# Layer two's channel norm on one Trainium2 core: centring folded into the dense weights, variance from sums of squares, the deviation spread as two bf16 products

## What is computed

```
def _L2_conv_ref(x, dw_w, dw_b, ln_g, ln_b, w1, b1, w2, b2, ls):
    y = conv7x7_depthwise(x, dw_w) + dw_b
    y = transpose(y, (0, 2, 3, 1))
    mu = mean(y, axis=-1, keepdims=True)
    var = mean(square(y - mu), axis=-1, keepdims=True)
    y = (y - mu) * rsqrt(var + 1e-5) * ln_g + ln_b
    h = gelu(einsum('btfc,hc->btfh', y, w1) + b1)
    y = einsum('btfh,ch->btfc', h, w2) + b2
    return transpose(y * ls, (0, 3, 1, 2))
```

## Time and profile before

| | |
|---|---|
| median of 3 runs | 3942.23 us (3942.04 to 3947.88) |
| the profiled execution's own time | 3944.25 us |
| its span, first to last instruction | 3942.5 us |
| mean granted TensorE clock | 0.941 of 2.4 GHz |
| busy share of the span | PE 87%, DVE 82%, ACT 55%, POOL 55% |
| layer two's stretches (four) | about 613 to 768, 1522 to 1683, 2432 to 2592 and 3341 to 3498 us |

### The profile page before, as it was taken

One profiled execution on the slowest core, in us unless ns is written; L12 is line 12 of the kernel. 1 busy time (PEld: TensorE's weight loads), 2 busy tenths in 40 slices (PEclk: granted clock), 3 DMA queues, 4 the chain that ended last, 5 costly groups with the idle time before them and its releaser, 6 DMA issues.

```text
span 3942.5 us, 78824 instructions
## 1 busy us (share of the span) xinstructions
PE 3422.8 (87%) x29499; PEld 2153.6 (55%) x29499; DVE 3218.1 (82%) x6755; ACT 2180.3 (55%) x4937; POOL 2150.4 (55%) x1888
## 2 busy tenths in 40 slices
PE   4999988989999998989999998988999998983555
PEld 1666643347667753336767753345776763343444
DVE  4999977769999967859999968859999977855666
ACT  2434432348888852338888862347888863232333
POOL 3455552447767523437767704437767715327775
PEclk9999999999999999999999999999999999995556
DMA  1000102065555412055555511045555521137775
GB/s 52 10 12 12 28 18 52 26 188 171 156 156 158 130 39 52 1 170 170 161 152 166 156 48 41 12 134 169 163 159 157 159 69 30 35 106 208 217 216 171
DMA packets 219932, 426.84 MB, mean 108 GB/s; under 512 B 27825, under 2 KB 126540, under 8 KB 217512
## 3 DMA queue, kind: packets, MB, share of 16 engines
q0 software_dynamic: 92160, 302.06, 25.9%
q1 hardware_dynamic: 127346, 119.80, 10.7%
q10 hardware_dynamic: 54, 0.01, 0.0%
HBM read 340.97 MB, written 60.71 MB: 102 GB/s over the span
## 4 chain that ended last, share of the span: by engine, by line
DVE 29%; PE 26%; POOL 8%; issue 7%; ACT 5%; DVEq 3%; SPq 2%; POOLq 0%; DMA 0%; ACTq 0%
DVE val L1331 7%; DVE mxc L1294 6%; DVE xl L1354 6%; PE bank L737 4%; POOL G L1794 4%; PE bank L598 3%; DVE val L1341 2%; PE bank L621 2%; PE bank L459 2%; DVE G L1485 2%; POOL reg L1794 2%; POOL x_cur L1794 1%; PE bank L559 1%; PE bank L811 1%; PE bank L562 1%
## 5 line engine op out<-in xcount | busy, mean ns | idle before, releaser
L1794 POOL DMA_INDIRECT G<-patch_table,idx x576 | 709.2, 1231 | 285.7 <-issue 165.6
L957 ACT ACTIVATE pt<-bank 128x512 f32<-128x512 f32 x1024 | 606.9, 593 | 322.5 <-DVE bank L1362 221.7
L598 PEld LDWEIGHTS bank<-vt,pt 128*128 128x128 bf16 x8192 | 548.1, 98 | 244.1 <-ACT pt L957 6.7
L1354 DVE TENSOR_TENSOR xl<-pt 128x512 bf16<-128x512 f32 (+1 forms) x1024 | 616.8, 603 | 60.4 <-PE bank L598 29.7
L1294 DVE TENSOR_REDUCE mxc<-bank 128x1 f32<-128x512 f32 x896 | 611.4, 684 | 32.2 <-PE bank L520 29.5
L598 PE MATMUL bank<-vt,pt 128*128 128x129 bf16 (+1 forms) x8192 | 633.7, 221 | 1.1 <-ACT osb L965 1.1
L598 PE MATMUL bank<-vt,xl 128*128 128x129 bf16 x4096 | 401.6, 221 | 10.7 <-DVE xl L1354 10.7
L1794 POOL DMA_INDIRECT reg<-patch_table,idx x256 | 302.3, 1181 | 115.5 <-issue 72.5
L1794 POOL DMA_INDIRECT x_cur<-patch_table,idx x256 | 303.2, 1184 | 103.7 <-issue 72.5
L520 PE MATMUL bank<-reg,qh 128*128 128x512 bf16 x896 | 342.2, 383 | 10.4 <-DVE mxc L1294 6.8
L1530 DVE SCALAR_TENSOR_TENSOR G<-xn,vec,G 128x512 f32<-128x512 f32 x384 | 305.0, 832 | 24.8 <-issue 20.4
(11 more groups left out here) (295 smaller groups left out, 7171.1 us busy)
## 6 DMA issues: line engine op xcount, KB each, us to landing
patch_table<-valt SPq DMA_DIRECT2D x64, 512.0 KB, 7.2
G<-patch_table,idx POOLq DMA_INDIRECT x576
x_cur<-in_x SPq DMA_DIRECT2D x4, 2048.0 KB, 8.8
xl<-in_x SPq DMA_DIRECT2D x32, 256.0 KB
attn_out<-ob SPq DMA_DIRECT2D x32, 256.0 KB, 2.9
x_store<-x_cur SPq DMA_DIRECT2D x4, 2048.0 KB, 6.5
xr<-x_store SPq DMA_DIRECT2D x32, 256.0 KB, 4.1
out<-fo SPq DMA_DIRECT2D x32, 256.0 KB
```

What stands on the lines that cost most here:

```text
L598: last = mm(O[t // 2][:, c0:c0 + width], image[:, at % ring, t * 128:(t + 1) * 128], vhl[:, values, st, 0:width], start=(st == 0 and part ...
L957: A(pt[:, at % PT_RING, :], ST[at % ST_RING] if n else ST_FIRST[at % 3], ACT.Exp, scale=SCALE).then_inc(s["exp_done"], 1)
L1354: v.tensor_tensor(pl[:, at % PL_RING, first:CH], pt[:, at % PT_RING, first:CH], ph[:, at % PT_RING, first:CH], ALU.subtract).then_inc(s["p ...
L1794: g.indirect_dma_start(out=patches(j, k), out_offset=None, in_=table[:], in_offset=bass.IndirectOffsetOnAxis(ap=idx[:, j * K1 + k:j * K1 + ...
```

## The change

The mean is no longer subtracted from y. Instead the weights of the first dense layer lose their mean over the input channels, and the conv's bias loses its own mean (setup: two more matmuls with `cavg` on PE, two subtractions on DVE, the scaling by `ln_g` moved ahead). The variance is E[y^2] - E[y]^2: PE makes both sums by one-column float32 matmuls (L760's kind, now eight in a row, at the place where L751 stood), ACT copies the first and squares the second, POOL subtracts, clamps at zero and adds epsilon, takes the power, and splits the 128x4 result in a high and a low bf16 part. ACT makes eight diagonals (bf16) in place of four (float32), and PE spreads them by two bf16 matmuls of 512 columns in place of one float32 one.

```diff
@@ PE, layer2 step
                     if norm:
                         pe.wait_ge(s["y_rdy"], B + 2)
-                        pe.wait_ge(s["ln_d"], B)
-                        mm(MX[0][:], cavg[:], y_chunk(1 - u), start=True, stop=True).then_inc(s["ln_m"], 1)
+                        pe.wait_ge(s["ln_ve"], B)
+                        for t in range(TB):
+                            mm(MX[1][:, TB + t:TB + t + 1], y_chunk(1 - u)[:, t * 128:(t + 1) * 128],
+                               cavg[:, 0:1], start=True, stop=True)
+                        pe.wait_ge(s["ln_sq"], B)
+                        for t in range(TB):
+                            last = mm(MX[1][:, t:t + 1], slots[:, L2SQ + (1 - u), t * 128:(t + 1) * 128],
+                                      cavg[:, 0:1], start=True, stop=True)
+                        last.then_inc(s["ln_v"], 1)
                     if conv:
                         taps(12, 22)
                     elif norm:
                         keep_busy(2, 7)
-                    if norm:
-                        pe.wait_ge(s["ln_sq"], B)
-                        pe.wait_ge(s["ln_ve"], B)
-                        for t in range(TB):
-                            last = mm(MX[1][:, t:t + 1], slots[:, L2SQ + (1 - u), t * 128:(t + 1) * 128],
-                                      cavg[:, 0:1], start=True, stop=True)
-                        last.then_inc(s["ln_v"], 1)
@@
                         pe.wait_ge(s["z_rdy"], B + 1)
-                        mm(TR[1][:], cavg[:], slots[:, L2DG + (1 - u), :], start=True, stop=True)\
+                        mm(TR[1][:], inverse_c, diagonal(1 - u)[:, 0, :], start=True, stop=False)
+                        mm(TR[1][:], inverse_c, diagonal(1 - u)[:, 1, :], start=False, stop=True)\
                             .then_inc(s["ln_bc"], 1)
@@ ACT, layer2 step
-                        act.wait_ge(s["ln_d"], B + 1)
+                        act.wait_ge(s["y_rdy"], B + 2)
                         A(slots[:, L2SQ + (1 - u), :], y_chunk(1 - u), ACT.Square).then_inc(s["ln_sq"], 1)
                     if norm:
                         act.wait_ge(s["ln_v"], B)
-                        A(ve4[:], MX[1][:, 0:TB], ACT.Identity, bias=eps[:]).then_inc(s["ln_ve"], 1)
+                        A(ve4[:], MX[1][:, 0:TB], ACT.Copy)
+                        A(mq4[:], MX[1][:, TB:2 * TB], ACT.Square).then_inc(s["ln_ve"], 1)
                     if norm:
                         act.wait_ge(s["ln_rs"], B)
                         act.wait_ge(s["z_rdy"], B)
-                        for t in range(TB):
-                            last = A(slots[:, L2DG + (1 - u), t * 128:(t + 1) * 128], ident[:], ACT.Copy,
-                                     scale=rs4[:, t:t + 1])
+                        for part, scales in enumerate((rh4, rl4)):
+                            for t in range(TB):
+                                last = A(diagonal(1 - u)[:, part, t * 128:(t + 1) * 128], ident[:], ACT.Copy,
+                                         scale=scales[:, t:t + 1])
                         last.then_inc(s["ln_dg"], 1)
@@ DVE, setup
             v.tensor_copy(xst[0:K1, 0, 0:C], P[1][0:K1, 0:C]).then_inc(s["b2_rows"], 1)
+            v.tensor_scalar(l2w1_s[:], l2w1_s[:], vec[:, LNG:LNG + 1], None, ALU.mult).then_inc(s["w1_scaled"], 1)
@@
-            v.tensor_scalar(l2w1_s[:], l2w1_s[:], vec[:, LNG:LNG + 1], None, ALU.mult)
+            dve.wait_ge(s["w1_mean"], 1)
+            v.tensor_tensor(l2w1_s[:], l2w1_s[:], P[2], ALU.subtract)
+            v.tensor_tensor(vec[:, DWB:DWB + 1], vec[:, DWB:DWB + 1], P[3][:, 0:1], ALU.subtract)
@@ DVE, layer2 step
-                        taps(0, 4)
-                    if norm:
-                        dve.wait_ge(s["ln_m"], B)
-                        v.tensor_tensor(y_chunk(1 - u), y_chunk(1 - u), MX[0][:], ALU.subtract)\
-                            .then_inc(s["ln_d"], 1)
-                    if conv:
-                        taps(4, dve_taps)
+                        taps(0, dve_taps)
@@ POOL, layer2 step
-                    g.tensor_tensor(rs4[:], ve4[:], mhalf[:].to_broadcast([128, TB]), ALU.pow)\
-                        .then_inc(s["ln_rs"], 1)
+                    g.tensor_tensor(ve4[:], ve4[:], mq4[:], ALU.subtract)
+                    pool.drain()
+                    g.tensor_scalar(ve4[:], ve4[:], 0.0, 1e-5, ALU.max, ALU.add)
+                    pool.drain()
+                    g.tensor_tensor(rs4[:], ve4[:], mhalf[:].to_broadcast([128, TB]), ALU.pow)
+                    pool.drain()
+                    g.tensor_copy(rh4[:], rs_high)
+                    g.tensor_tensor(rl4[:], rs4[:], rs_high, ALU.subtract).then_inc(s["ln_rs"], 1)
```

More of the change, by code:

```diff
@@ L110, in build @@
         mhalf = sb("mhalf", [128, 1])
-        eps = sb("eps", [128, 1])
         b1f = sb("b1f", [128, FT])
@@ L145, in build @@
         rs4 = sb("rs4", [128, TB])
+        mq4 = sb("mq4", [128, TB])
+        rh4 = sb("rh4", [128, TB])
+        rl4 = sb("rl4", [128, TB])
         bst = sb("bst", [128, NCH, 6])
@@ L205, in build, with diagonal @@
         tap_eye = w4f[:, 2 * TAP_W:2 * TAP_W + 32]
+        inverse_c = cavg[:].bitcast(BF16)[:, 1::2]
+        rs_high = rs4[:].bitcast(BF16)[:, 1::2]
+        def diagonal(u):
+            return slots[:, L2DG + u, :].bitcast(BF16).rearrange("p (s n) -> p s n", s=2)
         def y_chunk(u):
@@ L297, in build @@
             "t_ps t_ev in_ve in_pow in_ready relu_rdy tl_rdy l1w l1p l1s l1a l1f l1x "
-            "mlp_rdy zl_rdy hl_rdy tapw_in tapw_rdy tapw_out tapw_ld im0 im1 im2 im3 dwp y_rdy ln_m ln_d ln_sq ln_v ln_ve ln_rs ln_dg ln_bc z_rdy hp gl mo me xa "
+            "mlp_rdy zl_rdy hl_rdy tapw_in tapw_rdy tapw_out tapw_ld im0 im1 im2 im3 dwp y_rdy w1_scaled w1_mean ln_sq ln_v ln_ve ln_rs ln_dg ln_bc z_rdy hp gl mo me xa "
             "oc_ps oc_ev ot_ps ot_ev xs_rdy xt_ps xt_ev om_rdy em_rdy grid_rdy idx_rdy x3_out tbl_w "
@@ L453, in _ @@
             nc.tensor.transpose(P[1][0:K1, 0:C], vec[:, L1B:L1B + K1], ident[:]).then_inc(s["pe_setup"], 1)
+            pe.wait_ge(s["w1_scaled"], 1)
+            mm(P[2], cavg[:], l2w1_s[:], start=True, stop=True)
+            mm(P[3][:, 0:1], cavg[:], vec[:, DWB:DWB + 1], start=True, stop=True).then_inc(s["w1_mean"], 1)
             pe.wait_ge(s["dve_setup"], 1)
@@ L1190, in _ @@
             dve.sem_inc(s["y_rdy"], 2)
-            dve.sem_inc(s["ln_d"], 1)
             dve.sem_inc(s["xa"], 2)
@@ L1199, in _ @@
             v.memset(cavg[:], 1.0 / C)
-            v.memset(eps[:], 1e-5)
             dve.drain()
```

## The result

| | before | the changed kernel |
|---|---|---|
| median of 6 runs each | 3943.96 us (3939.08 to 3947.88) | 3960.00 us (3956.70 to 3964.90) |
| ratio to before, 95% interval | | 1.0042 (1.0031 to 1.0052) |
| profiled execution, own time | 3944.25 us | 3962.75 us |
| its span | 3942.5 us | 3961.0 us |
| mean granted TensorE clock | 0.941 | 0.938 |

What follows compares the result with a forecast made beforehand. PE was taken to bound the 17.17 us full step, DVE nearly so. Five full steps at +0.86 (4.3), steps 1 and 2 (0.4) and step 8 (1.1) gave 5.8 us an image, +23 over four: 3965 us, range 3936 to 3983.

Steps and rivals of the forecast that it cites:

- what would show it: Signs: POOL's five instructions about 4 us, PE idle 1 to 2 us before spreading, steps about 18.0, DVE waiting at z.
- POOL starts at 5.26: Full step: sums reach ACT at 4.76 us, two 128x4 instructions follow, then POOL's chain begins at 5.26.
- each link costs a whole tap, about 0.8: Full steps: each drained POOL instruction waits for DVE's tap to end, so each link costs about 0.8 us.
- Eight diagonals: ACT, full step: eight diagonals at 0.30 us each take 2.47 us against 1.28 for four, +1.19.
- PE's own work falls by 0.74: PE, full step: 0.13 us saved on the means and 0.61 on the spreading, 0.74 together.
- The clock falls: Rival: the granted clock drops in the full steps' new wait; given no chance of its own.
- Leave POOL free for the last links: Steps 1 and 2: DVE finishes its taps early, so POOL's last links run free; +0.2 us each.
- Its result matmuls lie under that: Step 8: the uncovered chain grows from 7.43 to 8.5 us, +1.1, and covers the result matmuls.
- The hidden chain: Rival: POOL's links slip between taps, DVE sets the step at 16.6 us, -12 us, 3930; chance 0.2.
- under about 2.6 us: Condition for the chain staying hidden: POOL's five instructions together take less than about 2.6 us.
- The 1.8 us that DVE would lose: If POOL held the shared ports through each instruction, DVE would lose some 1.8 us a step; not adopted.
- The half case: Rival: two links meet a tap, PE waits 0.5 us, -0.25 a step, +1.1 in step 8, 3942; chance 0.18.

Runs made afterwards that it cites:

- experiment 1: The changed kernel with the spreading put back to four float32 diagonals and one float32 matmul, without POOL's copy and last subtraction: 3938.34 us, ratio 0.9990.
- experiment 2: The kernel before with only the high/low bf16 split, eight diagonals and two bf16 spreading matmuls added: 3979.94 us, ratio 1.0095.
- experiment 5: The changed kernel with epsilon added by ACT and POOL's clamp instruction left out, one link fewer: 3930.91 us, ratio 0.9970.
- experiment 6: The changed kernel with clamp and epsilon as two drained POOL instructions, one link more: 3969.83 us, ratio 1.0067.
- experiment 3: The changed kernel with one of DVE's two tap accumulators moved from SBUF to PSUM: 3935.34 us, ratio 0.9978.
- experiment 11: The changed kernel with two idle matmuls in step 8 where PE waits for ACT's square: 3958.89 us, ratio 1.0035.
- experiment 4: The changed kernel with 14 idle matmuls ahead of step 1's wait for the diagonals: 3956.04 us, ratio 1.0039.

## Why the prediction was right, and where it was right by luck

**The mechanism was right.** POOL's chain grew past PE's arrival: its five instructions span 3.78 us in full steps and 2.25 in step 8, PE and DVE wait where "what would show it" had them wait, and experiments 1 and 2 put the loss on it. Two of the signs missed in size: PE waits less than 1 us, and the steps are 17.46, not 18.0. DVE's saved subtraction bought nothing, as forecast. The setup shows nothing either: image 0's first joining starts at 628.51 us, at 628.32 before.

**The wait was put at 1.6 us and is 0.81 to 0.95.** The prediction's two large terms in the full step were both too large.

- "POOL starts at 5.26": it starts at 5.04. ACT's two 128x4 take 0.24 together in place of 0.26 + 0.17, as neither has the bias operand of L1089 (0.17 against 0.26).
- "each link costs a whole tap, about 0.8": the chain took 3.78 and not 4.14. I had every link ask inside a tap. L1776 asks in the gap between pairs and takes 0.23. The model of turns was right and the count of missed turns one too high; experiments 5 and 6 show that this count can't be carried by a price for each link.
- Eight diagonals: 2.47 forecast, 2.44 measured.
- "PE's own work falls by 0.74": it is 0.59, the difference between 17.17 and the 16.58 of experiment 3, in which the chain is hidden. Experiment 1 gives 0.07 of it to the means (0.13 forecast), which leaves 0.52 for the spreading (0.61 forecast).

The first two moved the diagonals' end from 11.9 to 11.29 in the step; they start the spreading at 11.35 instead of 12.0. PE arrives at 10.54, where 10.4 was forecast. With 17.46 against the 16.58 of the hidden chain, the wait costs 0.88, and the step grew by 0.88 - 0.59 = 0.29 us where 0.86 had been forecast. This is the term that failed: 17.2 us for steps 3 to 7, of which 6.1 came.

**Steps 1 and 2 were put at +0.2 an image each and the clock at nothing.** "The clock falls" was among the rivals, for the full steps only, where it indeed stayed at 1.00. I didn't look at the step in which PE already stood for 3 us. There the longer chain lengthened an uncovered wait by about 0.8 us, some 3 us over four images. What the clock adds varies: the time at half clock behind that wait was 6.8 us over four images before, 20.5 in the changed kernel's execution and 6.8 again in experiment 11's, and step 1 grew by 8.9 and by 3.1. "Leave POOL free for the last links" was wrong for step 2 in three images of four: POOL's chain took 4.1 to 4.3 us there, PE stood 1.1 to 1.3 us before the spreading, and the step grew by 0.7 to 0.8; in image 2, with a chain of 3.2, it shrank by 0.3. Together +0.5 an image.

**Step 8 was put at +1.1 an image and is +1.41.** Its chain runs as forecast: squares to ACT 1.09 (1.1), POOL 2.25 (2.37), diagonals 2.45 (2.5). "Its result matmuls lie under that" was wrong. Timeline of PE there, after:

```profile
1677.23 1.05 PE L767 MATMUL bank<-cavg,G 128*128 128x1 f32 x8 [0.51 <-ACT G L1098]
1678.15 2.72 PE L470 MATMUL bank<-l1w_s,identb 128*128 128x512 bf16 x7
1680.66 0.63 PE L780 MATMUL bank<-valt,l2w_s 128*128 128x512 bf16 x1
...
1683.99 0.38 PE L790 MATMUL bank<-G,cavg 128*128 128x512 bf16 x1
```

The seven idle matmuls behind the sums run at half clock, 2.72 us for before's 1.67, the results start late, and the spreading waits for them 0.6 us behind the last diagonal (1683.37). Where the clock held (experiment 11, and two images of experiment 4), joining to z took 11.14, +0.87. So 0.54 of the +1.41 is the clock's.

**The rivals.** The hidden chain (3930, given 0.2) is not what this kernel does, but is what it does when one link is taken out: "under about 2.6 us" for POOL's chain was about the right condition: experiments 3 and 5 at 2.26 and 2.25 us give 3935 and 3931, and in experiment 3 the steps with a chain of 2.65 us still take 16.58 while those with 3.26 take 16.95. The 1.8 us that DVE would lose to a POOL holding the ports through each instruction didn't come: DVE's pairs beside the links keep 1.41 to 1.43 us. The half case had a wait of 0.5 us and a step of -0.25; the truth lies between it and my forecast. Its sum would have been 3942, since it too left out the clock. The 3965 came near the 3960 by luck in its parts: the full steps' 11 us too much stand against steps 1, 2 and 8, which came out higher than forecast, by some 5 us with experiment 11's step 1 and by 10 with the changed kernel's, in which the omitted clock has its full share.

## What to carry to other kernels

When a chain of small instructions lies beside a busy engine that can hold it up, place its requests in that engine's rhythm before pricing them; better, give one of that engine's operands another memory, which here took 1.5 of 3.8 us off the chain at no cost. When a chain is lengthened, look first at those steps in which nothing hides it, and at the granted clock behind each wait there: what is lost behind the wait can be more than the wait, and it can differ from one execution to the next, so one trace of each kernel doesn't price it. Check the parts of a forecast apart, since a total can agree by two errors.

## What the runs showed of the hardware that I had not expected

- POOL's 128x4 instructions take 0.20 (two tensors), 0.24 (tensor and scalars), 0.19 (copy) and 1.03 us (power) when nothing holds them up, and mostly 0.5 to 0.7 for the small ones that start inside one of DVE's taps with two SBUF inputs. They don't lengthen those taps (1.41 to 1.43 a pair), while POOL's 128x512 instructions do (1.61 for one tap).
- A float32 tap on DVE whose sum lives in PSUM is as fast as one with it in SBUF (0.75 and 0.75 us), and is untouched by POOL: all 208 of them in experiment 3 took 0.75 to 0.76.
- TensorE's granted clock, in step 1, fell behind waits of 2.9 to 3.5 us in four images of four (experiment 5) and 3.0 us in two of four (before), and held behind 3.7 and 3.8 us in two (experiment 11). One kernel's step 1 so differs by nearly 5 us between its own images (18.10 and 22.85 in the changed kernel).
- In step 8 it fell from 1.00 to 0.50 with no idle time above 0.51 us, behind one-column float32 matmuls and that wait, in 19 of 36 images. With a 512-column float32 matmul and seven idle ones ahead of the sums, it held in 12 of 12.
